# Router logits from uncentred rows, and half of the routing work moved in among the fusion products

## The reference, cut to what matters

```python
h = h + (concat(h_fwd, h_bwd) @ fusion_W + fusion_b)       # fusion
x = (h - mean(h)) / sqrt(var(h) + 1e-5)                    # layer norm over 256 features
probs = softmax(x @ gate_w.T)                              # gate_w: 8 x 256
w, idx = top_k(probs, 2); w = w / sum(w)
out = sum over experts e of combine[:, e] * (silu(x @ Wg[e]) * (x @ Wu[e]) @ Wd[e])
```

## Time and profile before

| | us |
|---|---|
| median of 3 runs | 440.19 (440.14 to 440.54) |
| profiled execution, its own time | 441.06 |
| span of that execution | 439.3 |
| PE busy | 409.6 (93%) |
| DVE busy | 204.9 (47%) |
| ACT busy | 148.3 (34%) |
| POOL busy | 103.1 (23%) |

### The profile page before, as it was taken

How to read it: one execution, slowest core, us unless ns; L and a number is a source line. 1 busy time by engine, 2 the same in 40 slices (tenths; PEclk the granted TensorE clock), 3 DMA queues, 4 the chain that set the end, 5 groups by cost and what they waited for, 6 DMA issues and landing times.

```text
span 439.3 us, 6649 instructions
## 1 busy us (share of the span) xinstructions
PE 409.6 (93%) x2593; PEld 344.6 (78%) x2593; DVE 204.9 (47%) x438; ACT 148.3 (34%) x321; POOL 103.1 (23%) x126
## 2 busy tenths in 40 slices
PE   6999999999999989998999999869999999898895
PEld 4787888888778979988989889847774487677784
DVE  0326688888846224243243332401207379624452
ACT  1124666666315112121121121100554224227642
POOL 2012555444312722021020220220100400002440
PEclk9989999999996999999999999979999999999989
DMA  7999990000000256857658560117000000000001
GB/s 252 352 298 298 393 354 7 1 1 0 2 0 1 81 143 241 265 139 238 207 133 298 153 188 10 19 25 246 0 1 0 0 1 4 2 0 0 1 1 54
DMA packets 30613, 48.45 MB, mean 110 GB/s; under 512 B 2160, under 2 KB 26864, under 8 KB 28528
## 3 DMA queue, kind: packets, MB, share of 16 engines
q1 hardware_dynamic: 28208, 45.17, 31.4%
q0 software_dynamic: 2368, 2.80, 4.2%
HBM read 38.90 MB, written 9.05 MB: 109 GB/s over the span
## 4 chain that ended last, share of the span: by engine, by line
PE 72%; DMA 8%; DVE 6%; issue 6%; ACT 4%; POOL 3%; SPq 1%; POOLq 0%
PE bank L596 13%; PE bank L713 11%; PE bank L730 9%; DMA wg<-slots 7%; PE bank L481 6%; PE bank L486 5%; PE bank L500 3%; PE bank L792 3%; PE bank L559 3%; PE bank L781 3%; PE bank L912 3%; PE bank L574 2%; PE bank L845 2%; POOL slots L433 2%; PE bank L521 1%
## 5 line engine op out<-in xcount | busy, mean ns | idle before, releaser
L713 PE MATMUL bank<-tt,wup 128*128 128x192 f32 x512 | 86.9, 327 | 0.7 <-ACT tt L1023 0.7
L713 PEld LDWEIGHTS bank<-tt,wup 128*128 128x128 f32 x512 | 83.1, 191 | 0.9 <-issue 0.9
L1331 DVE TENSOR_TENSOR scratch<-bank,scratch 128x192 f32<-128x192 f32 x64 | 22.8, 356 | 86.6 <-ACT scratch L1038 86.6
L596 PE MATMUL bank<-gru_x,wg 128*128 128x288 f32 x192 | 50.8, 408 | 0.0
L444 POOL DMA_INDIRECT mixed<-wg,token x16 | 22.6, 1412 | 115.0 <-DVE wg L1345 112.5
L481 PE MATMUL bank<-zero 128*128 128x288 bf16 (+1 forms) x266 | 44.5, 313 | 3.8 <-issue 3.8
L399 POOL TENSOR_TENSOR rm<-ve,half_neg 96x3 f32<-96x3 f32 x24 | 20.5, 856 | 116.0 <-DVE ve L1170 109.1
L1038 ACT ACTIVATE scratch<-bank 128x192 f32<-128x192 f32 x64 | 21.1, 330 | 70.7 <-PE bank L713 70.7
L596 PEld LDWEIGHTS bank<-gru_x,wg 128*128 128x128 f32 x192 | 35.6, 190 | 8.8
L481 PEld LDWEIGHTS bank<-zero 128*128 128x128 bf16 (+1 forms) x266 | 28.3, 110 | 12.3 <-issue 4.1
L416 POOL TENSOR_TENSOR sq<-sq 128x288 f32<-128x288 f32 x14 | 26.0, 1857 | 21.5 <-ACT sq L956 21.5
(11 more groups left out here) (217 smaller groups left out, 642.8 us busy)
## 6 DMA issues: line engine op xcount, KB each, us to landing
wup<-w_up SPq DMA_DIRECT2D x8, 2048.0 KB, 7.8
wdn<-w_down SPq DMA_DIRECT2D x8, 1024.0 KB, 6.3
slots<-empty SPq DMA_DIRECT2D x2, 2385.0 KB, 19.9
wg<-w_gru SPq DMA_DIRECT2D x4, 1024.0 KB, 11.4
wup<-w SPq DMA_DIRECT2D x2, 1024.0 KB, 8.9
xp<-patches SPq DMA_DIRECT2D x6, 288.0 KB, 5.3
wg<-slots SPq DMA_DIRECT2D x16, 99.4 KB, 5.3
xp<-w_qkv SPq DMA_DIRECT2D x1, 1536.0 KB, 16.2
```

The source lines that it names most:

```text
L596: last = pe.matmul(bank[:, 2 * g + m, 0:NT], wg[:, l, d, g, k, m * P:(m + 1) * P], src, start=(k == 0), stop=(k == KH - 1))
L713: last = pe.matmul(bank[:, 2 + m % 4, g * 256:g * 256 + C], wup[i][:, k, g * I + m * P:g * I + (m + 1) * P], xg[i][:, k, :], start=(k == 0 ...
L1331: dve.tensor_tensor(gt[m % 2], bank[:, 2 + m % 4, 0:C], sg[m % 2], ALU.mult).then_inc(s_vact[c], 1)
```

## The change

The mean is no longer taken out of the rows for the logits. The mean of the gate weights over the features is taken out of the weights instead (`GATE_MEAN`, a product of the averaging matrix with `wr`, and a subtraction on DVE), which gives the same logits from `h`. With that, the first half's mean and logits stand between `fuse(1, 1)` and `fuse(1, 2)`. The transposes are split by half, and so are ACT's copies, with one signal for each tile. On DVE the centring of half 1 moves into the chain on the logits, `ln_eps(19)` moves from its sixth place to behind the eleventh, and `prs` moves behind the scan. The six warm-ups ahead of the rank products are gone.

```diff
@@ PE @@
             stay_warm(4, 2)
+            pe.wait_ge(s_load["wr"], 16)
+            pe.wait_ge(s_cen, LN_MOE - 1)
+            for k in range(KH):
+                last = pe.matmul(bank[:, 7, GATE_MEAN:GATE_MEAN + E], avg[:], wr[:, k, :], start=(k == 0), stop=(k == KH - 1))
+            last.then_inc(s_wrm, 1)
             ln_square(LN_MOE - 2)
...
             fuse(1, 0)
             fuse(1, 1)
+            def logits(n):
+                pe.wait_ge(s_hf, n + 1)
...
+            def turn_rows(n):
+                pe.wait_ge(s_cen, LN_MOE + n + 1)
...
+            pe.wait_ge(s_hf, 1)
+            ln_mean(LN_MOE, h[:, :, half(0)])
+            pe.wait_ge(s_wrc, 1)
+            logits(0)
             pe.wait_ge(s_norm, LN_MOE)
             fuse(1, 2)
             fuse(1, 3)
...
-            for n in range(2):
-                pe.wait_ge(s_hf, n + 1)
-                ln_mean(LN_MOE + n, h[:, :, half(n)])
-            logits(0)
             ln_square(LN_MOE)
+            turn_rows(0)
             logits(1)
+            ln_mean(LN_MOE + 1, h[:, :, half(1)])
+            turn_rows(1)
             ln_square(LN_MOE + 1)
-            for j in range(6):
...
-            stay_warm(6, 3)
             pe.wait_ge(s_msk, 1)
...
-                pe.wait_ge(s_xt, 3)
+                pe.wait_ge(s_xt, 6)
@@ ACT @@
-            for n in range(2):
-                squares(LN_MOE + n)
...
+            squares(LN_MOE)
+            keep_rows(0)
+            squares(LN_MOE + 1)
             sc_.wait_ge(s_max, 1)
             sc_.activation(ex[:], prs[:], ACT.Exp).then_inc(s_exp, 1)
...
+            keep_rows(1)
@@ DVE @@
             ln_center(LN_MOE - 1)
+            dve.wait_ge(s_wrm, 1)
+            dve.tensor_tensor(wr[:], wr[:], bank[:, 7, GATE_MEAN:GATE_MEAN + E].rearrange("p (k e) -> p k e", k=1)
+                              .broadcast_to([P, KH, E]), ALU.subtract).then_inc(s_wrc, 1)
...
-            for n in range(2):
-                add_fused(n)
-            for n in range(2):
-                ln_center(LN_MOE + n)
+            add_fused(0)
+            ln_center(LN_MOE)
+            add_fused(1)
             ln_eps(LN_MOE)
```

More of the change, by code:

```diff
@@ L35 @@
 MASKED = -1e30
+GATE_MEAN = 8
 C = 192
@@ L189, in stat_bank, with row_bank, row_col @@
             return 6
+        def row_bank(j):
+            return 2 * (j // JT) + j % JT // 2
+        def row_col(j):
+            return j % JT % 2 * H
         def half(n):
@@ L429, in _ @@
             for j in range(6):
-                if j % 2 == 0:
-                    pool.wait_ge(s_xt, j // 2 + 1)
+                pool.wait_ge(s_xt, j + 1)
                 for k in range(2):
@@ L637, in _ @@
             fuse(1, 1)
+            def logits(n):
+                pe.wait_ge(s_hf, n + 1)
+                for j in range(n * JT, (n + 1) * JT):
+                    for k in range(KH):
+                        last = pe.matmul(bank[0:TT, 5, j * E:(j + 1) * E], h[:, k, j * TT:(j + 1) * TT], wr[:, k, :],
+                                         start=(k == 0), stop=(k == KH - 1))
+                last.then_inc(s_logit, 1)
+            def turn_rows(n):
+                pe.wait_ge(s_cen, LN_MOE + n + 1)
+                for j in range(n * JT, (n + 1) * JT):
+                    for m in range(KH):
+                        last = pe.transpose(bank[0:TT, row_bank(j), row_col(j) + m * P:row_col(j) + (m + 1) * P],
+                                            xn[:, m, j * TT:(j + 1) * TT], ident[:])
+                    if j % JT >= 1:
+                        last.then_inc(s_xtp, 1)
+            pe.wait_ge(s_hf, 1)
+            ln_mean(LN_MOE, h[:, :, half(0)])
+            pe.wait_ge(s_wrc, 1)
+            logits(0)
             pe.wait_ge(s_norm, LN_MOE)
@@ L1002, in _, with keep_rows @@
                     squares(LN_GRU + it - 1)
-            for n in range(2):
-                squares(LN_MOE + n)
+            def keep_rows(n):
+                sc_.wait_ge(s_pow, LN_MOE + n + 1)
+                for j in range(n * JT, (n + 1) * JT):
+                    if j % JT != 1:
+                        sc_.wait_ge(s_xtp, 2 * n + j % JT // 2 + 1)
+                    sc_.activation(xtok[:, j, 0:H], bank[0:TT, row_bank(j), row_col(j):row_col(j) + H], ACT.Identity,
+                                   scale=rmoe[:, j:j + 1], bias=0.0).then_inc(s_xt, 1)
+            squares(LN_MOE)
+            keep_rows(0)
+            squares(LN_MOE + 1)
             sc_.wait_ge(s_max, 1)
             sc_.activation(ex[:], prs[:], ACT.Exp).then_inc(s_exp, 1)
[L1009 to L1012, removed]
-                last = sc_.activation(xtok[:, j, 0:H], bank[0:TT, j // 2, j % 2 * H:(j % 2 + 1) * H], ACT.Identity,
-                                      scale=rmoe[:, j:j + 1], bias=0.0)
-                if j % 2 == 1:
-                    last.then_inc(s_xt, 1)
+            keep_rows(1)
             sc_.activation(awake[:], mean_h[0:1, :], ACT.Sigmoid)
@@ L1293, in _ @@
             link(dve, dve.tensor_tensor(keys[:], keys[:], ranks[:], ALU.mult))
-            dve.wait_ge(s_pow, LN_MOE + 2)
-            dve.tensor_tensor(prs[:], pr[:], over(rmoe), ALU.mult).then_inc(s_max, 1)
             link(dve, dve.tensor_reduce(mx1[:], by_tile(keys[:]), AX_X, ALU.max))
+            ln_eps(LN_MOE + 1)
             link(dve, dve.tensor_tensor(sel[:, 1], keys[:], over(mx1), ALU.is_equal))
@@ L1300, in _ @@
                                    msk[:].rearrange("p e j -> p (e j)"), 0.0, ALU.mult, ALU.add).then_inc(s_msk, 1)
+            dve.wait_ge(s_pow, LN_MOE + 2)
+            dve.tensor_tensor(prs[:], pr[:], over(rmoe), ALU.mult).then_inc(s_max, 1)
             dve.wait_ge(s_exp, 1)
```

17 lines of the change are left out of this document (2 added, 15 removed).

## The result

| | before | after |
|---|---|---|
| median of 20 runs each, same chip, us | 440.32 (438.03 to 443.48) | 442.73 (440.44 to 446.06) |
| ratio after/before, 95% interval | | 1.0053, 1.0031 to 1.0074 |
| profiled execution, its own time | 441.06 | 442.89 |
| its span | 439.3 | 441.1 |

The change costs 0.53%, 1.4 to 3.3 us by the interval. The profiled execution of before lies 0.7 us above the median of its 20 runs, that of after 0.2 above. Ratios in this text leave out executions that ran disturbed, and medians take in all, so a kernel can have the lower median and still a ratio above 1. The page of after hides where the cost is: PE's busy sum grows by 0.4 us, and the clock row has a dip again in the slices of the routing, as in the earlier trace rows.

What follows compares the result with a forecast made beforehand. The scatter path from `place` to expert 1's rows was taken as the bound, the PE path 0.77 us behind. `place` 0.6 us later, shift +0.6 to +0.9, half to all staying: 440.19 + 0.4 = 440.6 us, range 438.3 to 442.2.

Steps and rivals of the forecast that it cites:

- no change: Whole kernel: a time within 0.2% of before, between 439.31 and 441.07 us, chance 0.44.
- case A: Routing: the exponential's chain replaces the warm-ups as what `place` waits for; +0.3 to +0.9 us stays, 440.6 us, chance 0.40.
- 141.45, against 140.86: End of `place` in the routing, summed through norm 19's steps and the exponential: 0.6 us later than before.
- (a): Routing, theory of the experiments: cost of the later `place` and gather, set by norm 19 and the exponential; forecast +0.6 us at `place`.
- If the clock rises 3.4 us later: Gather: clock up only at 144.8, so 2.9 us of it at half speed, 1.45 us more; routing's shift 0.9 us.
- 0.77 us of slack: Ahead of expert 1's transposes: the PE path (gather, expert 0) is 0.77 us behind the leading scatter path.
- half of the shift stays: Sixty warm-ups behind the last expert: with the clock's rise fixed at 298.4, 0.75 us of shift become 0.4.
- B: Routing: clock falls at 134.6 as before, half 1's transposes and variance at half speed; +2.1 us at `place`, 441.3 to 442.3, chance 0.30.
- C: Sixty warm-ups behind the last expert: all at full speed, 7.45 us; 438.4 us, 436.7 at the bottom, chance 0.22.
- D: Routing: norm 19's steps overlap better, `place` up to 0.8 us earlier, 439.4 to 440.2 us, chance 0.08.
- (b): Gather, theory of the experiments: cost of running it at half clock; the prediction had 1.45 us as an upper bound.

Runs made afterwards that it cites:

- e12: The changed kernel, unedited, with all scatters, run again on a later chip: 444.49 us, ratio 1.0023 to before.
- e3: The changed kernel with the first half's mean and logits behind the fusion products again: 446.91 us, ratio 1.0055 to before.
- e4: The changed kernel with half 1's mean ahead of its logits, both ahead of half 0's transposes, to begin norm 19 early: 446.07 us, ratio 0.9995 to before.
- e1: The changed kernel with the six warm-ups put back ahead of the rank products: 444.91 us, ratio 0.9981 to before.
- e8: e4 with the six warm-ups of e1 put back: 445.23 us, ratio 0.9982 to before.
- e11: e1 with only the scatters of the first choice, six of twelve: 439.83 us, ratio 0.9899 to before.
- e17: e1 with POOL pausing ahead of the seventh scatter, all twelve kept: 442.76 us, ratio 0.9941 to before.
- e2: The kernel before with only its six warm-ups removed: 444.77 us, ratio 1.0000 to before.
- e7: e2 again on another chip, beside a control: 445.32 us, ratio 0.9993 to before.
- e6: The changed kernel, unedited, on the same chip as the control e5: 445.1 us, ratio 0.9994 to before.
- e10: The changed kernel with only the scatters of the first choice, six of twelve: 441.87 us, ratio 0.9951 to before.
- e16: The changed kernel with POOL pausing ahead of the seventh scatter for chunk 1 of expert 0's up product: 444.87 us, ratio 0.9987 to before.
- e9: The kernel before with only the scatters of the first choice, six of twelve: 437.88 us, ratio 0.9858 to before.
- e5: The kernel before, unedited, as a control on a later chip: 445.0 us, ratio 0.9993 to before.
- e18: e13 again, unedited, beside e16 and e17 on the same chip: 441.67 us, ratio 0.9931 to before.
- e13: The kernel before with POOL pausing ahead of the seventh scatter for chunk 3 of expert 0's up product: 441.19 us, ratio 0.991 to before.

## Why the prediction was wrong

The forecast was "no change", 440.6 us, with 442.2 as the upper end; it came out at 442.73, slower.

**What held.** The way to the second `add_fused`: 2.44 us predicted, 2.42 measured (done at 11.19 and 13.61). The gate mean took 0.36 us, from 121.22 to the next record at 121.58, within the bounds of 0.32 to 0.45, and DVE's subtraction was hidden. The ranks no longer hold `place`; the exponential's chain does. The scan came at 19.75, 0.66 us later than in before, where 0.8 was forecast; `place` at +0.48 against a forecast of +0.6; the gather's start at +0.2. All that is case A's mechanism, read correctly from the order and the durations.

**First failed step: the yardstick for `place`.** The sum "141.45, against 140.86" takes the 140.86 from one execution, in which the clock fell 15.8 us after the mean, ahead of the transposes. Of seven profiles with before's order and its warm-ups, `place` was done at 21.21 or 21.22 in four (the clock fell at 16.5) and at 22.07 to 22.38 in three. With after's order it was 22.54 or 22.55 in seven of eight, e12 the exception, with its clock at half speed in the fusion products. So (a) is +0.5 us against the execution that I read and +1.3 against the commoner one, in runs on the later chips; of the first measurement there is one profile of before, so which one was common there is not shown. The working said that the clock decides; it drew that doubt for the changed kernel only, not for the one it subtracted.

**Second failed step: the gather's clock.** The forecast priced the gather at half speed as the upper end of A ("If the clock rises 3.4 us later"), 1.45 us, and let the 0.77 us of slack take half of it. The term was too small and stood at the wrong place, in the upper bound and not in the sum: the gather took 1.92 us more in after, and 1.8 to 3.3 in the five profiles of the changed kernel. It happened in every profile of the new order without the six warm-ups: 5.99, 7.37, 7.28, 6.24 and 5.94 us, and in e3 and e4, against 4.07 to 4.14 in seven profiles of before. With six back it was 4.14 in all four (e1, e8, e11, e17). Before's order without the six has 4.47 and 4.14 (e2, e7), so neither edit does it alone. What the new order moves is the fall: it came at 19.2 to 20.1 in after, e6, e10 and e16, and not at about 16 as with before's. What the six change is the stay. Without them the clock stayed at half speed for 6.8 to 10.2 us, into the gather. In e1 and e11, with the six, it fell at 19.4 all the same but was back after 3.4 us, ahead of the gather, and in e17 it did not fall there. The Trainium skill (TensorE: Matmul & The Clock Gate, "Why this matters for your kernels") ties drops to idle gaps between bursts of matmuls. The longer stay without the six agrees with that in kind, though the idle stretches here, 0.92 and 0.95 us, are shorter than the gaps that its row names. For the earlier fall in before, with PE busy, the trace does not agree, and I had let that disagreement speak for both.

**Third failed step: "half of the shift stays".** The timeline of PE behind the last expert, before and then after:

```profile
303.08 1.16 PE L763 MATMUL bank<-ident,wg 96*128 96x96 f32 x12
```

```profile
295.06 10.01 PE L489 MATMUL bank<-zero 128*128 128x288 bf16 x60 [3.64 <-issue]
304.90 1.16 PE L780 MATMUL bank<-ident,wg 96*128 96x96 f32 x12
```

Counted from the mean, the sixty warm-ups start 1.01 us later in after (175.38 against 174.37) and the transposes behind them 0.92 later (185.22 against 184.30): nearly all of the shift stayed, because the clock's rise moved along, to 300.16 from 298.43, 0.8 us later by the same count. The prediction had that as the other bound ("If the rise moves along, all of d stays") and took the half. From e9 to e10 the block gave back 0.91 of 4.61 us (10.03 against 9.12 us), a fifth; another 1.2 went behind it, where e9 has the clock at half speed from 416.4 to 419.8 and e10 has it at full. Of 4.47 us at expert 1's transposes 2.49 are left at the end of the span (439.1 − 118.77 against 437.8 − 119.96).

**The other cases.** B's 441.3 to 442.3 lay closest, and the upper end of 442.2 comes from it, but its cause did not occur: PEclk was 1.00 at 134.5 in after. That the range missed by 0.5 us only is therefore luck. C did not occur in any profile: the sixty took 8.8 to 10.5 us each time, never 7.45. D neither; half 1's centring started at 136.08.

**The sum now.** (a) 1.3 and (b) 1.8 to 3.3 us at expert 1, with about 2 given back by the end in e9 and e10, make roughly 1 to 3 us. The first measurement gave 2.4. That one is without the stall, so its split into (a) and (b) is inferred from e9, e10 and e11 on another chip, and not measured there. Its own pair of profiles has 0.21 us at the gather's start and 1.92 in the gather, less the 0.77 of slack: 1.36 at the transposes, and 0.9 at the end; that the other executions of before had the earlier `place` is an inference.

**Open.** Why the sigmoids stand still while POOL issues scatters, what the two share, and why the two profiles of the first measurement do not show it. The trace puts the wait down to PE's finished bank or to an unknown source. No packet of the instruction queues lies inside the stall of e5 (the nearest are at 136.1 and 162.0 us), so a late load of instructions is not it.

## What to carry to other kernels

Subtract like from like: where the clock falls close to a stage, one profile of the kernel before is one draw, and two or three of them show which draw it was. Warm-ups that look like an obstacle ahead of a result may be what keeps the next large product at full clock; before they go, ask what fills the idle time that their absence leaves. And when a change costs time on one chip and none on another, look in the unchanged kernel for a stall that hides it, remove that, and measure the pair again.

## What the runs showed of the hardware

- A run of indirect scatters on POOL, one each 1.24 us, held back ACT's sigmoids, which don't depend on them, in runs on five chips: by 5.7 us in e5 and 5.1 in e6. The two profiles of the first measurement have the same twelve scatters and no such wait. The first late one was due 7.9 to 10.6 us behind the start of the first scatter in e1 to e8. Six scatters (e9 to e11) did nothing, nine 3 us, and a pause of 2 us after the sixth removed all (e17, e18) or all but 1.4 us (e13). The Trainium skill (SBUF — State Buffer, "Who interferes with whom") says that DMA never contends with a compute engine and names POOL's descriptor writing as the victim of a DVE operation. Here DVE had nothing to do in the stall, and it was ACT that waited; the runs don't show through what.
- The same kernel took 440.3 us in the median in the first measurement and 445.2 to 446.0 on the five chips of the later ones.
- The half-speed stretch of the clock behind the fusion products began 15.5 to 16.5 us behind the mean in seven profiles of the same kernel's order, and `place` was done at 21.2 where it began at 16.5 and lasted 3.4 us, at 22.1 to 22.4 where it began by 15.8 and lasted 6.8.
